# Gated delta rule on one core: the 16x16 diagonal blocks of all chunk matrices regrouped through a DRAM scratch whose chunk matrices are laid out with a skewed stride

## What is computed

```python
k_beta = k * beta
attn = -(einsum('bhcid,bhcjd->bhcij', k_beta, k) * decay_mask)   # 64 x 64 per chunk
attn = where(upper, 0.0, attn)                                     # strictly lower
def _correct_row(a, i):                                            # forward substitution
    row = a[..., i, :]
    corr = einsum('...j,...jk->...k', row, a) * (arange(64) < i)
    return a.at[..., i, :].set(row + corr), None
attn, _ = lax.scan(_correct_row, attn, arange(1, 64))
attn = attn + eye(64)                                              # (I + A)^-1
value_corrected = attn @ v_beta
k_cumdecay = attn @ (k_beta * g_exp)
```

## Time and profile before

| | us |
|---|---|
| median of 3 runs | 5653.62 |
| lowest and highest | 5644.02, 5666.7 |
| the profiled execution, its own time | 5670.83 |
| its span in the trace | 5668.7 |
| TensorE busy in the span | 4973.4 (88%) |
| VectorE, ScalarE busy | 3513.1 (62%), 3046.6 (54%) |
| mean granted clock of TensorE | 0.948 of full speed |

### The profile page before, as it was taken

One profiled execution on the slowest core, in us unless ns is written; L12 is line 12 of the kernel. 1 busy time (PEld: TensorE's weight loads), 2 busy tenths in 40 slices (PEclk: granted clock), 3 DMA queues, 4 the chain that ended last, 5 costly groups with the idle time before them and its releaser, 6 DMA issues.

```text
span 5668.7 us, 144560 instructions
## 1 busy us (share of the span) xinstructions
PE 4973.4 (88%) x52244; PEld 3458.8 (61%) x52272; DVE 3513.1 (62%) x6423; ACT 3046.6 (54%) x7910; POOL 1063.6 (19%) x1064
## 2 busy tenths in 40 slices
PE   3899999999779999999977999999997899999898
PEld 1566666666556666666645666666664566666666
DVE  6466666666446666666645666666664666666665
ACT  2355555555346555555524655555552555555555
POOL 0022221222111212221211221222220122221122
PEclk7899999999989999999988999999998999999999
DMA  2121222222122221222112222212211221222221
GB/s 68 48 57 42 58 56 53 59 48 53 39 53 54 58 59 43 56 57 54 42 38 59 56 58 53 59 42 58 57 34 44 70 56 46 56 57 54 53 49 38
DMA packets 685930, 296.71 MB, mean 52 GB/s; under 512 B 598976, under 2 KB 642112, under 8 KB 675648
## 3 DMA queue, kind: packets, MB, share of 16 engines
q1 hardware_dynamic: 685120, 286.09, 21.0%
HBM read 213.55 MB, written 59.78 MB: 48 GB/s over the span
## 4 chain that ended last, share of the span: by engine, by line
PE 62%; DVE 11%; ACT 9%; issue 8%; SPq 5%; DMA 3%; DVEq 0%; POOL 0%; ACTq 0%; POOLq 0%
PE pj L587 10%; PE dsb L724 8%; PE ms L645 7%; SPq L409 5%; PE pj L582 4%; ACT arena L856 4%; PE pot L682 4%; PE pot L653 4%; DVE cy L1135 4%; PE dsb L696 3%; PE pod L665 3%; PE ms L600 3%; PE pod L708 2%; PE ms L614 2%; PE pj L577 2%
## 5 line engine op out<-in xcount | busy, mean ns | idle before, releaser
L587 PE MATMUL pj<-xnT,wt 128*128 128x512 f32 x2048 | 1037.2, 636 | 101.0 <-ACT arena L856 58.7
L1135 DVE SCALAR_TENSOR_TENSOR cy<-xpad,cw,cy 128x1024 f32<-128x1024 f32 x768 | 1059.7, 1386 | 33.3 <-ACT cy L876 23.7
L1374 POOL TENSOR_TENSOR rout<-rin,expo 128x2 f32<-128x2 f32 x512 | 366.8, 716 | 2738.7 <-DVE rin L1270 2738.7
L724 PE MATMUL dsb<-wo,yT 128*128 128x256 f32 x2048 | 609.6, 423 | 98.5 <-issue 94.3
L587 PEld LDWEIGHTS pj<-xnT,wt 128*128 128x128 f32 x2048 | 369.1, 198 | 528.4 <-issue 372.7
L1368 POOL TENSOR_TENSOR sdec<-st,gel 128x512 f32<-128x512 f32 x384 | 402.2, 1047 | 1047.5 <-DVE st L1259 866.2
L875 ACT ACTIVATE xpad<-pj 128x512 f32<-128x512 f32 x512 | 302.5, 591 | 500.5 <-PE pj L587 499.7
L934 ACT ACTIVATE yT<-dsb 128x256 f32<-128x256 f32 x512 | 196.2, 383 | 644.6 <-PE dsb L715 643.2
L582 PE MATMUL pj<-wt,xnT 128*128 128x256 f32 x2048 | 511.7, 393 | 0.0
L724 PEld LDWEIGHTS dsb<-wo,yT 128*128 128x128 f32 x2048 | 365.9, 199 | 217.7 <-issue 180.5
L1249 DVE SCALAR_TENSOR_TENSOR rr<-pot,nge,arena 128x128 f32<-128x128 f32 x896 | 271.2, 344 | 338.6 <-PE pot L653 338.6
(11 more groups left out here) (163 smaller groups left out, 8502.6 us busy)
## 6 DMA issues: line engine op xcount, KB each, us to landing
qge<-ge_rows SPq DMA_DIRECT2D x64, 1024.0 KB, 7.0
wt<-in_L_attn_W_qkvz SPq DMA_DIRECT2D x64, 768.0 KB, 4.4
gb<-g_rows SPq DMA_DIRECT2D x128, 256.0 KB, 4.1
a_d<-at SPq DMA_DIRECT2D x64, 512.0 KB, 2.6
wo<-in_L_attn_W_out SPq DMA_DIRECT2D x64, 256.0 KB, 2.7
x_d<-xpair SPq DMA_DIRECT2D x128, 128.0 KB, 1.7
ap_<-a_d SPq DMA_DIRECT2D x512, 16.0 KB, 1.8
dd<-x_d SPq DMA_DIRECT2D x512, 16.0 KB, 1.8
```

What stands on the lines that cost most here:

```text
L587: last = mm(pj[n % 2][:, :], wt[:, k, col:col + DH], batch(xnT, k, i), start=(k == 0), stop=(k == KD - 1))
L724: last = mm(dsb[:, 0, GRP * DH:GRP * DH + D], yT[:, h, :], wo[:, p, h, :], start=(h == 0), stop=(h == GRP - 1))
L1135: stt(y, x[:, :, tap:tap + SEQ], cw[:, kind, tap:tap + 1], y, ALU.mult, ALU.add).then_inc(S["conv"], 1)
L1374: tt(rout[:, :], rin[:, :], expo[:, 0, 0:GRP], ALU.pow).then_inc(S["routs"], 1)
```

## The change

Both scratches become flat arrays in which row p of unit u begins at p * 128 + u * 8256 elements (ROW = 128, UROW = 64 * 128 + 64). Since 8256 is four times 2064 and 2064 is 16 * 128 + 16, one step of 2064 elements leads from a diagonal block to the next one, over the four blocks of a unit and on to the next unit. So `diagonal(t, b)` names the 64 diagonal blocks of sequence b as one access pattern with 64 outer steps, and `whole(t)` names the full [128, 16, 64] tile in rows of 64 elements.

- `at` is written to `a_d` through `whole`: 2048 runs of 256 bytes, where there were 128 runs of 4 KB.
- `ap_` is filled by two gathers (one for each half of the partitions) in place of eight. The blocks lie in other partitions than before, and all that VectorE does with them is the same.
- `xi` and `xit` are each written by two scatters of 1024 runs of 64 bytes, where there was one write of 128 runs of 1 KB.
- `dd` and `ee` are each read by one transfer of the whole tile, zeros included: 2048 runs of 256 bytes, 512 KB, where there were eight transfers of 256 runs of 64 bytes, 128 KB together.
- `x_d` becomes two arrays. Their zeros are written once at the start from the zeroed `dd` and `ee`, and SP waits for that.
- `off` and its six transfers stay.

```diff
+        UROW = CH * ROW + CH
+        a_d = dram("a_d", [P * ROW + U * UROW])
+        x_d = [dram(f"x_d{n}", [P * ROW + U * UROW]) for n in range(2)]
...
+        def whole(t):
+
+            return bass.AP(tensor=t.tensor, offset=t.offset, ap=[[ROW, P], [UROW, U], [1, CH]])
+
+        def diagonal(t, b):
+
+            return bass.AP(tensor=t.tensor, offset=t.offset + b * CH * ROW,
+                           ap=[[UROW // NBLK, U * NBLK], [ROW, BLK], [1, BLK]])
...
+            sp.wait_ge(o_dve, 1)
+            for n, t in enumerate((dd, ee)):
+                sp.dma_start(whole(x_d[n]), t[:, :, :]).then_inc(d_zero, 16)
+            sp.wait_ge(d_zero, 32)
             sp.wait_ge(q_ev, 12)
...
-                for r in range(GRP * NBLK):
-                    src = a_d[r * BLK:(r + 1) * BLK, :, (r % NBLK) * BLK:(r % NBLK + 1) * BLK]
-                    sp.dma_start(ap_[r * U:(r + 1) * U, :, :], src.rearrange("j u i -> u j i")).then_inc(d_a, 16)
+                for b in range(NB):
+                    sp.dma_start(ap_[half(b), :, :], diagonal(a_d, b)).then_inc(d_a, 16)
...
-                sp.dma_start(x_d[:, 0], xi).then_inc(d_x0, 16)
+                for b in range(NB):
+                    sp.dma_start(diagonal(x_d[0], b), xi[half(b)]).then_inc(d_x0, 16)
                 after(sp, "sub", g, 18)
                 apart(sp)
-                sp.dma_start(x_d[:, 1], xit).then_inc(d_x1, 16)
+                for b in range(NB):
+                    sp.dma_start(diagonal(x_d[1], b), xit[half(b)]).then_inc(d_x1, 16)
                 for n, (dst, done) in enumerate(((dd, d_dd), (ee, d_ee))):
-                    loaded(sp, (d_x0, d_x1)[n], g, 1)
+                    loaded(sp, (d_x0, d_x1)[n], g, NB)
                     apart(sp)
-                    for r in range(GRP * NBLK):
-                        sp.dma_start(dst[r * BLK:(r + 1) * BLK, :, (r % NBLK) * BLK:(r % NBLK + 1) * BLK],
-                                     x_d[r * U:(r + 1) * U, n].rearrange("u j i -> j u i")).then_inc(done, 16)
+                    sp.dma_start(dst[:, :, :], whole(x_d[n])).then_inc(done, 16)
```

More of the change, by code:

```diff
@@ L42 @@
 ENGINES = 5
+ROW = P
 def shape_constants():
@@ L72, in build @@
         cols_d = dram("cols_d", [HK, P, COLS * U])
-        a_d = dram("a_d", [P, U, CH])
-        x_d = dram("x_d", [P, 2, BLK, BLK])
+        UROW = CH * ROW + CH
+        a_d = dram("a_d", [P * ROW + U * UROW])
+        x_d = [dram(f"x_d{n}", [P * ROW + U * UROW]) for n in range(2)]
         wgu_d = dram("wgu_d", [P, KD * 2 * FFN], BF16)
@@ L196, in build @@
         d_w, d_g, d_ge, d_wo, d_q = sem("d_w"), sem("d_g"), sem("d_ge"), sem("d_wo"), sem("d_q")
-        d_a0, d_a, d_off, d_x0, d_x1, d_dd, d_ee = (sem(n) for n in ("d_a0", "d_a", "d_off", "d_x0", "d_x1", "d_dd", "d_ee"))
+        d_zero, d_a0, d_a, d_off, d_x0, d_x1, d_dd, d_ee = (sem(n) for n in ("d_zero", "d_a0", "d_a", "d_off", "d_x0", "d_x1", "d_dd", "d_ee"))
         phase = sem("phase")
@@ L382, in relayout @@
                 apart(sp)
-                sp.dma_start(a_d, at[:, :, :]).then_inc(d_a0, 16)
+                sp.dma_start(whole(a_d), at[:, :, :]).then_inc(d_a0, 16)
                 loaded(sp, d_a0, g, 1)
                 apart(sp)
-                for r in range(GRP * NBLK):
-                    src = a_d[r * BLK:(r + 1) * BLK, :, (r % NBLK) * BLK:(r % NBLK + 1) * BLK]
-                    sp.dma_start(ap_[r * U:(r + 1) * U, :, :], src.rearrange("j u i -> u j i")).then_inc(d_a, 16)
+                for b in range(NB):
+                    sp.dma_start(ap_[half(b), :, :], diagonal(a_d, b)).then_inc(d_a, 16)
                 before(sp, "pp", g)
@@ L619, in off_products @@
                 if n == 0:
-                    loaded(pe, d_dd, g, GRP * NBLK)
+                    loaded(pe, d_dd, g, 1)
                     loaded(pe, d_off, g, NB * (NBLK - 1))
@@ L635, in fixpoint @@
                 if r == 0:
-                    loaded(pe, d_ee, g, GRP * NBLK)
+                    loaded(pe, d_ee, g, 1)
                     after(pe, "pneg", g, n + 1)
@@ L1198, in invert_rows @@
                 if r0 == 1:
-                    loaded(dve, d_a, g, GRP * NBLK)
+                    loaded(dve, d_a, g, NB)
                     before(dve, "yp", g)
```

## The result

| | before | after |
|---|---|---|
| median, us | 5655.99 | 5754.43 |
| ratio (95% interval) | 1 | 1.0162 (1.0123 to 1.0200) |
| profiled execution, us | 5670.83 | 5732.23 |
| its span | 5668.7 | 5730.1 |
| mean granted clock of TensorE | 0.948 | 0.945 |

The changed kernel is 1.6% slower, some 92 us by the ratio, where 51 us less were forecast. One of the four executions of the changed kernel took 10539.84 us at a mean granted clock of 0.482; it counts in the median above and not in the ratio. Line 629 of the kernel before is line 643 now, 645 is 659, and the transfers of the way back are lines 416, 420 and 424.

What follows compares the result with a forecast made beforehand. TensorE's waits for dd and ee, 91.1 us, were taken as the bound; gains of 39 (woven dd waits), 10 (ee) and 2.4 us (fronts), 51 together, off the 5653.6 us median gave 5602 us, range 5560 to 5676.

Steps and rivals of the forecast that it cites:

- What bounds the kernel: TensorE's waits for dd (line 629, 79.2 us) and ee (line 645, 11.9 us), together 91.1 us, 1.6% of the span.
- The price of the scatters: Way back: xi's two scatters, issued at 1096.32 and 1096.80, land at 1099.13 (1.36 us packets, 1.45 fixed).
- The sign I had named: Changed profile: scatters landing above 3.5 us, or dd above 5, would show the first two rivals (dear scatters, dear read).
- Instruction packets: Dear-read rival: the read of dd now and then runs beside a 16 KB instruction packet; no time was given.
- The price of the whole read: Reads of dd and ee: 2.45 us of packets at 19 ns each, plus 1.63 us fixed.
- forecast gain of 0.66 us: Line 629, woven pass: TensorE waits 0.40 us for dd in place of 1.06.
- Packet price: DMA: a 64-byte scatter packet taken at 10.6 ns, upper end 19; a 256-byte read packet at 19 ns.
- the scatters are dear: Rival, way back: at 19 ns a packet dd lands 0.92 us late, 5697 us; 17% together with reads beyond 25 ns.
- The waits for `ee`: Line 645: ee lands at 1106.1, ahead of 1109.5, so all waits should go; 10 of 11.9 us counted.
- The forward half: First relayout, write of at and two gathers: 0 us gained, margin before VectorE from 3.8 to 4.6 us.
- the zeroing: Start: two 512 KB writes, 6.4 us on SP, under a 27.1 us wait: 0 us, or 6.4 once if uncovered.
- The four fronts: Unwoven passes: dd lands at 254.04 against 254.71, 0.6 us gained four times, 2.4 us.

Runs made afterwards that it cites:

- The last version: Kernel before, with xit written from ScalarE's queue and ScalarE also issuing the last two of dd's eight reads: ratio 0.9856, 5593.3 against 5681.3 us.

## Why the prediction was wrong

**What bounds the kernel: right.** The wait for `dd` at line 629 was the place, a us there reaches the end, and what can be won there is small. The last version won it. The bound of 91.1 us left out the clock, though: that version's profile has 61 us less of these waits, and its span is 78.5 us shorter, for TensorE is also busy for 28 us less.

**The price of the scatters: the step that failed.** The sum let the second scatter of `xi` follow the first by 0.48 us, the distance of two plain writes in the earlier trace rows, and `xi` land at 1096.32 + 1.36 + 1.45, 2.81 us after the first issue. From the changed kernel's view of `xpair` (min, median, max in ns), with 128 issues in each row, and the landing of line 416's transfers:

```profile
L416 SPq DMA_DIRECT2D x_d<-xpair x128: 632/656/677, 246.2 to 5650.3; - x128
L420 SPq DMA_DIRECT2D x_d<-xpair x128: 574/672/1602, 247.7 to 5652.1; - x128
```

```profile
DMA to landing us min/median/max: 2.5/2.6/4.8
```

A scatter of 1024 runs holds SP for 0.66 us, so the second goes out 0.69 us after the first, and it lands 2.6 us after that: `xi` is there at 3.29 us in the median, and the read of `dd` goes out 0.09 us later. The plain write was there at 1.72. SP's own work isn't what ends last: its fourth scatter is issued by 3.16 us, and with the scatters of `xit` out of the way the read still went out at 3.38. A write of 128 runs had 0.35 us, and a read of 256 runs has 0.45: the time grows with the runs, and the rows of the copies to `off`, at 0.61 us an issue, would have warned me. Duration of an issue is a price of its own, and I had taken it from the cheapest shape. Of the 0.8 us by which a single scatter lands later than the plain write it is 0.3; what the rest is, no run separates. The sign I had named, a landing of the scatters above 3.5 us, isn't in the median, and is there in the 17 passes.

**Instruction packets: a term put at nothing.** I named the 16 KB packets only as a risk to the read and gave them no time. In 17 of 60 woven passes one holds up a scatter of `xi`, which lands at 4.6 to 5.5 us. Before, the landing had 0.63 us to spare; the change took that away. So the read went out 1.04 us later in the median and 1.52 in the mean, where I had forecast 0.47.

**The price of the whole read: the second step.** Alone the read lands after 4.2 us (`ee` in the experiment with the read ahead of `xit`), and my price was 2.45 + 1.63 = 4.08. It starts slowly, but at the full rate of 290 GB/s a packet takes 256 x 16 / 290 = 14 ns and not 19. What was wrong is the overlap: with `xit` ahead of it I expected 4.50 us and measured 4.9, for the read of `ee`, which I let queue behind `dd`, shares the engines with it (5.0 in the old write with whole reads, where no scatter ran). The fit of 2.0 us and the bytes at 436 GB/s that I quoted is stated by the Trainium skill, DMA: Bandwidth & Descriptors, Anatomy of one DMA, for transfers issued from GpSimd. These are issued from SP, so its 3.2 us was no forecast for them. And TensorE starts 0.23 us after the landing, in the median before and after; the sum had nothing for that, so a third of the forecast gain of 0.66 us was never there.

**The clock: missing.** The text has no term for it. The rows of the kernel before had it: in the earlier trace rows the 64 matmuls behind a wait of 5.82 us took 3.68 us, in the earlier trace rows behind 1.06 us they took 2.08. I quoted both and didn't compare them. With a median wait that goes from 1.0 to 1.7 us, and to 2.9 in the 17 passes, many passes end where it matters.

**Packet price: right, and the rival with it half.** From 949.9 to 951.7 us only the scatters of `xi` run in the changed kernel:

```profile
DMA packets 1966, 0.12 MB, mean 69 GB/s; under 512 B 1966, under 2 KB 1966, under 8 KB 1966
...
q1 hardware_dynamic: 1966, 0.12, 56.5%
```

That is 0.565 x 1.8 x 16 / 1966 = 8.3 ns a packet, under the 10.6 that I took by the same working. So the rule of the Trainium skill on read-modify-write below 512 bytes (DMA: Bandwidth & Descriptors, Specifications), which spoke for the rival, shows no cost in the packets' time here. The rival "the scatters are dear" had the right culprit and sign, but by their issue and their landing and not by the packets' time; its 5697 us fell short of 5754.

**Sum.** From the first scatter to TensorE's start I forecast 2.86 + 4.50 = 7.36 us in a woven pass. The 43 common ones have 3.40 + 4.93 + 0.23 = 8.57 (means): 0.54 by the scatters, 0.43 by the read, 0.23 by TensorE's start. The kernel before had 8.02. So these passes lose 0.55 us each where 0.66 were to be won, and the 17 with an instruction packet lose 1.83. In all, the woven passes wait 55 us longer where 39 were to be won, and the slower matmuls add 25. The waits for `ee` went, 11.9 us for the 10 forecast. The forward half cost nothing, as forecast: VectorE waits for no gather in either profile. Nor did the zeroing, for the first write of `xi` goes out at 246.2 us, 247.2 before. The four fronts wait 4 us longer where 2.4 were to be won: the first 5.81 us, as before, the others 5.87, 3.35 and 3.35.

## What to carry to other kernels

When small transfers are merged, count the queue's issue time for each new shape before the data's: a transfer of 1024 short runs holds the queue for about twice as long as one of 128, and it both lands later and sits ahead of everything the queue must do next. Look at the slack of each landing too: one that nothing waits for can take an instruction packet on its engines, and one at the head of the chain can't. A median hides that; compare means, or look at the worst passes. Where an engine waits for the last of several issues, start the chain earlier, or give part of it to a second queue whose engine is idle then; that won here what the layout lost. And price a wait on TensorE by what the matmuls behind it take as well.

## What the runs showed of the hardware

A read of 2048 runs of 256 bytes from DRAM lands 4.2 us after its issue with no other transfer of the kernel beside it, 4.4 with scatters right behind it, and 5.0 with a second such read behind it; the write of the same shape lands after 3.8. It takes about a us until the read runs at full rate. A scatter packet of 64 bytes to DRAM takes 8.3 ns. One 16 KB instruction packet (0.9 to 1.4 us on one engine) makes a scatter of 1024 runs land 1.3 to 2.2 us later. An issue isn't a fixed price of its shape either: the same scatter holds SP for 0.66 us, and for 1.18 behind a whole read. Behind idle times of TensorE of about 2 us, in the middle of dense work, the granted clock fell in some passes and in others with nearly the same wait it didn't (0.73 and 1.00 behind 2.07 and 1.99 us above). Over all runs the shortest such wait with slow matmuls behind it was 1.86 us, the longest without was 3.60 (last experiment, a front; clock 1.00), which is why a mean wait says little about what a longer wait costs.
